# Queries' rests on GpSimd, the last tile's sums on VectorE, and first passes in front of the scores of their round

## The reference

```
h = ln(x, g1, be1);  x = attn(h, h, Wq1, Wk1, Wv1, Wo1, bo1) + x        # self attention, 1024 keys
h = ln(x, g2, be2);  x = attn(h, context, Wq2, Wk2, Wv2, Wo2, bo2) + x  # cross attention, 64 keys
h = ln(x, g3, be3);  a, gate = split(h @ Wp + bp)
x = a * gelu(gate) @ W2 + b2 + x

attn: 16 heads of 64; softmax(q k^T / 8) v, heads joined, @ Wo + bo
```

## Time and profile before

| | us |
|---|---|
| median of 3 runs | 1987.01 |
| profiled execution, own time | 1986.85 |
| its span, first to last instruction | 1985.1 |
| an ordinary chunk: score stage, products, slot | 9.27 + 7.09 + 3.14 |
| TensorE, VectorE, ScalarE, GpSimd busy | 1971.6, 1393.6, 1150.6, 1444.1 |

### The profile page before, as it was taken

The page is one execution under the profiler, slowest core; times in us unless marked ns, Lnnn a source line. Parts: engine busy times, 40 slices in busy tenths (PEclk is TensorE's granted clock), DMA queues, the critical chain, the costliest instruction groups (busy, mean ns, idle before and its releaser), DMA issues.

```text
span 1985.1 us, 32079 instructions
## 1 busy us (share of the span) xinstructions
PE 1971.6 (99%) x12056; PEld 1345.1 (68%) x12056; DVE 1393.6 (70%) x2382; ACT 1150.6 (58%) x2042; POOL 1444.1 (73%) x752
## 2 busy tenths in 40 slices
PE   9999999999999999999999999999999999999999
PEld 7555655667565556755655666565569999888888
DVE  6688687666768786587687666767867888744443
ACT  6665576565556665465666555656756766533332
POOL 3699899978979997899799798979896665200000
PEclk9999999999999999999999999999999999999999
DMA  7301000011000000020000001010030420000100
GB/s 256 138 38 64 17 22 22 12 33 54 22 12 12 33 12 33 1 75 11 11 12 22 33 12 54 22 33 1 22 106 22 150 65 1 1 22 33 33 11 32
DMA packets 40506, 77.63 MB, mean 39 GB/s; under 512 B 5920, under 2 KB 29600, under 8 KB 38304
## 3 DMA queue, kind: packets, MB, share of 16 engines
q1 hardware_dynamic: 40352, 75.59, 11.5%
HBM read 51.46 MB, written 24.12 MB: 38 GB/s over the span
## 4 chain that ended last, share of the span: by engine, by line
PE 92%; DVE 3%; POOL 3%; issue 1%; ACT 1%; POOLq 0%; DVEq 0%
PE score L577 21%; PE score L556 18%; PE score L703 9%; PE attn_project L512 8%; PE attn_project L688 5%; PE attn_project L717 5%; PE score L524 5%; PE score L658 4%; PE score L626 3%; PE attn_project L538 3%; PE first_score L538 3%; PE score L562 3%; POOL acc L1528 2%; PE first_score L672 1%; PE first_score L588 1%
## 5 line engine op out<-in xcount | busy, mean ns | idle before, releaser
L1528 POOL TENSOR_TENSOR acc<-acc,pT 128x1024 f32<-128x1024 f32 x384 | 916.7, 2387 | 54.4 <-POOL acc L1528 0.9
L1271 ACT ACTIVATE pT<-score 128x1024 f32<-128x1024 f32 x512 | 515.7, 1026 | 89.1 <-PE score L562 53.5
L556 PE MATMUL score<-qk 64*128 64x512 f32 x3072 | 467.5, 405 | 2.5 <-DVE hT L852 1.9
L577 PE MATMUL score<-pT,vT 128*64 128x512 f32 x1952 | 432.3, 595 | 0.0
L556 PEld LDWEIGHTS score<-qk 64*128 64x128 f32 x3072 | 267.2, 184 | 97.0 <-ACT pT L1271 20.9
L907 DVE TENSOR_REDUCE nmax<-first_score 128x2 f32<-128x1024 f32 x256 | 311.0, 1215 | 2.4 <-PE first_score L538 2.4
L907 DVE TENSOR_REDUCE nmax<-attn_project 128x2 f32<-128x1024 f32 x256 | 311.0, 1215 | 1.0 <-PE attn_project L538 0.9
L577 PEld LDWEIGHTS score<-pT,vT 128*64 128x64 f32 x1952 | 134.7, 137 | 259.5 <-issue 252.6
L1525 POOL TENSOR_TENSOR acc<-pT 128x1024 f32<-128x1024 f32 x64 | 153.4, 2396 | 68.6 <-ACT pT L1271 68.6
L512 PE MATMUL attn_project<-hT,wqk 128*128 128x512 f32 x738 | 186.3, 401 | 0.0
L703 PE MATMUL score<-hT,wp 128*128 128x512 f32 x768 | 183.7, 395 | 0.0
(11 more groups left out here) (201 smaller groups left out, 3007.2 us busy)
## 6 DMA issues: line engine op xcount, KB each, us to landing
wqk<-wqk_parts SPq DMA_DIRECT2D x24, 512.0 KB, 3.3
xres<-x_middle SPq DMA_DIRECT2D x10, 512.0 KB, 3.7
raw_v<-in_L_xattn_Wv SPq DMA_DIRECT2D x8, 512.0 KB, 4.9
keys_all<-keys SPq DMA_DIRECT2D x1, 4096.0 KB, 13.1
values_all<-values SPq DMA_DIRECT2D x1, 4096.0 KB, 13.2
wqk_parts<-wqk SPq DMA_DIRECT2D x8, 512.0 KB, 3.3
out_x<-xres SPq DMA_DIRECT2D x7, 512.0 KB, 3.0
xres<-in_x SPq DMA_DIRECT2D x3, 1024.0 KB, 5.7
```

Source lines behind the costliest of these rows:

```text
L556: last = e.matmul(bank, key_part(P, h, r, jt), queries1[P % 2][r, w, c * BANK:(c + 1) * BANK], start=(fresh and part == 0), stop=(not fres ...
L577: last = e.matmul(banks[bank][head * DH:(head + 1) * DH, :], vT[:, v_slot(D, jt), c0:c0 + DH], pT[:, jt, head, :], start=(jt == 0), stop=( ...
L1271: e.activation(pT[:, jt].rearrange("p h n -> p (h n)"), SC[R % 2][:, :], ACT.Exp).then_inc(s.exponential, 1)
L1528: e.tensor_tensor(total, total, pT[:, jt], ALU.add).then_inc(s.probs_added, 1)
```

## The change

- **First passes.** Each round issues its first pass of the next chunk in front of its scores, where it issued it behind them. The passes themselves, their banks and the number of row maxima stay.
- **Queries' rests.** But for the first three units, ScalarE copies the scaled projection of the queries in fp32 from PSUM to SBUF, into the place that their rest will take, and this copy alone frees bank PJ. One chunk later ScalarE rounds it from SBUF (round_queries, between the shift and write_oT), and GpSimd subtracts in place (split_queries, at the end of its chunk). VectorE no longer takes part. The whole keys are kept in the place of their rests too, where a tile of their own held them.
- **The last tile's sums.** GpSimd adds seven tiles with six additions. VectorE folds the eighth tile by itself (fold_last, behind the transposes of the maxima, in front of fold_sums). The product that sums over partitions takes both, 64 columns, and VectorE adds the two halves (totals) in front of the reciprocals.

```diff
         maxima = sb("maxima", [PART, 2, SQUARE])
-        keys_full = sb("keys_full", [PART, BANK // 2])
         QB = BANK // SQUARE
         quads = sb("quads", [PART, PART])
-        folded = sb("folded", [PART, 2 * QB])
+        folded = sb("folded", [PART, 3, 2 * QB])
+        totals = sb("totals", [PART, 2 * QB])
         rsum = sb("rsum", [PART, QB])
...
             ("wo1", [PAIRS, DIM], F32R))
+        _, qk1_whole, _, qk0_whole = overlay(
+            ("before_qk", [PRING * N + 3 * TILES * BANK + (2 * ARING + 1) * BANK], F32), ("qk1_whole", [4 * N + BANK], F32),
+            ("sums_between", [2 * BANK], F32), ("qk0_whole", [4 * N + BANK], F32))
         PAIR = BANK // 2
+        queries_whole = [tile[:, N:2 * N] for tile in (qk0_whole, qk1_whole)]
+        keys_whole = [tile[:, 2 * N:3 * N].rearrange("p (c n) -> p c n", c=CHUNKS) for tile in (qk0_whole, qk1_whole)]
         queries1 = [tile[:, 0:2 * N].rearrange("p (w n) -> p w n", w=2) for tile in (qk0, qk1)]
...
         keys_of = numbered((P, u) for P in range(B * PAIRS) for u in range(CHUNKS))
+        queries_of = numbered((P, u) for P in range(B * PAIRS) for u in range(2, 2 + CHUNKS))
+        FIRST_QUERIES = [(0, 2), (0, 3), (1, 2)]
+
+        def queries_rest(unit):
+
+            if unit in FIRST_QUERIES:
+                return s.first_queries_lo, queries_of[unit]
+            return s.queries_lo, queries_of[unit] - len(FIRST_QUERIES)
...
             return jobs + [("out1", *tile, through[i % len(through)]) for i, tile in enumerate(out1_tiles(C))]
+
+        def queries_unit(C):
+
+            P, c = divmod(C, CHUNKS)
+            return [(P + 1 + c, 3 - c)] if C >= 0 and P + 1 + c < B * PAIRS else []
...
                 last.then_inc(s.qk_projected, 1)
-                free[bank] = ((s.split_lo, qk_of[P, u]),)
+                free[bank] = ((s.split_lo, keys_of[P, u]) if u < 2 else queries_rest((P, u)) if (P, u) in FIRST_QUERIES
+                              else (s.queries_kept, queries_of[P, u] - len(FIRST_QUERIES)),)
...
                 bank = PASS_BANKS[head][half]
-                need.wait_ge(s.split_hi, qk_of[P, 2 + c])
+                need.wait_ge(s.queries_hi, queries_of[P, 2 + c])
                 need.wait_ge(s.keys_rounded, keys_of[P, half])
...
                 if part < len(TERMS):
-                    for u in (2 + c, jt // TPC):
-                        need.wait_ge(s.split_hi, qk_of[P, u])
-                        need.wait_ge(s.split_lo, qk_of[P, u])
+                    need.wait_ge(s.queries_hi, queries_of[P, 2 + c])
+                    need.wait_ge(*queries_rest((P, 2 + c)))
+                    need.wait_ge(s.split_hi, keys_of[P, jt // TPC])
+                    need.wait_ge(s.split_lo, keys_of[P, jt // TPC])
                     if part == 0:
...
                 need.wait_ge(s.acc_folded, C + 1)
+                need.wait_ge(s.last_folded, C + 1)
                 need.wait_ge(s.quads_made, 4)
                 bank_free(bank)
-                e.matmul(banks[bank][:, 0:2 * QB], quads[:, :], folded[:, :], start=True, stop=True
-                         ).then_inc(s.summed, 1)
-                free[bank] = ((s.sum_inverted, C + 1),)
+                both = folded[:, 0:2] if C % 2 == 0 else folded[:, 0:3:2]
+                e.matmul(banks[bank][:, 0:4 * QB], quads[:, :], both, start=True, stop=True).then_inc(s.summed, 1)
+                free[bank] = ((s.sum_totalled, C + 1),)
...
                         sum_quads(C - 1, "T0")
+                    if C + 1 < NC:
+                        for head in range(2):
+                            first_score(*next_part(C + 1, jt), head)
                     for part in range(len(TERMS) + (jt % TPC < 2)):
...
                             score(TILES * C + jt, part, head)
-                    if C + 1 < NC:
-                        for head in range(2):
-                            first_score(*next_part(C + 1, jt), head)
                 for jt in range(TILES):
...
+            def fold_last(C):
+
+                need.wait_ge(s.exponential, TILES * (C + 1))
+                need.wait_ge(s.summed, C - 1 if C > 1 else 0)
+                e.tensor_reduce(folded[:, 1 + C % 2], pT[:, TILES - 1].rearrange("p h (b n) -> p (h b) n", n=SQUARE), AX.X,
+                                ALU.add, apply_transpose=True).then_inc(s.last_folded, 1)
+
             def fold_sums(C):
-                need.wait_ge(s.probs_added, (TILES - 1) * (C + 1))
+                need.wait_ge(s.probs_added, ADDS * (C + 1))
                 need.wait_ge(s.summed, C)
-                e.tensor_reduce(folded[:, :], acc[:, C % ARING].rearrange("p h (b n) -> p (h b) n", n=SQUARE), AX.X, ALU.add,
+                e.tensor_reduce(folded[:, 0], acc[:, C % ARING].rearrange("p h (b n) -> p (h b) n", n=SQUARE), AX.X, ALU.add,
                                 apply_transpose=True).then_inc(s.acc_folded, 1)
...
                 need.wait_ge(s.summed, C + 1)
+                e.tensor_reduce(totals[:, :], banks[bank][:, 0:4 * QB].rearrange("p (w q) -> p q w", w=2), AX.X, ALU.add
+                                ).then_inc(s.sum_totalled, 1)
+                need.wait_ge(s.sum_totalled, C + 1)
                 for head in range(2):
                     r = slice(head * DH, (head + 1) * DH)
-                    last = e.reciprocal(rsum[r, :], banks[bank][r, head * QB:(head + 1) * QB])
+                    last = e.reciprocal(rsum[r, :], totals[r, head * QB:(head + 1) * QB])
                 last.then_inc(s.sum_inverted, 1)
...
                 for job in jobs:
-                    if job[0] == "qk":
-                        split_qk(*job[1:])
+                    if job[0] == "qk" and job[2] < 2:
+                        change_keys(*job[1:])
                     elif job[0] == "sum":
...
                     turn_max(C + 1)
+                if C + 1 < NC:
+                    fold_last(C)
                 if C == NC - 1:
...
                 if u >= 2:
-                    e.activation(queries1[P % 2][:, 0, (u - 2) * BANK:(u - 1) * BANK], banks[bank], ACT.Copy, scale=SCALE
-                                 ).then_inc(s.split_hi, 1)
+                    span = slice((u - 2) * BANK, (u - 1) * BANK)
+                    if (P, u) in FIRST_QUERIES:
+                        e.activation(queries1[P % 2][:, 0, span], banks[bank], ACT.Copy, scale=SCALE
+                                     ).then_inc(s.queries_hi, 1)
+                    else:
+                        e.activation(queries_whole[P % 2][:, span], banks[bank], ACT.Copy, scale=SCALE
+                                     ).then_inc(s.queries_kept, 1)
                     return
                 need.wait_ge(s.keys_changed, keys_of[P, u] - 1)
-                e.copy(keys_full[:, :], banks[bank][:, 0:PAIR]).then_inc(s.keys_copied, 1)
+                e.copy(keys_whole[P % 2][:, u, PAIR:], banks[bank][:, 0:PAIR]).then_inc(s.keys_copied, 1)
                 e.copy(keys_hi[P % 2][:, u, PAIR:], banks[bank]).then_inc(s.keys_rounded, 1)
...
                 e.copy(keys_hi[P % 2][:, u, 0:PAIR], banks[bank][:, PAIR:]).then_inc(s.split_hi, 1)
+
+            def round_queries(P, u):
+                span = slice((u - 2) * BANK, (u - 1) * BANK)
+                need.wait_ge(s.queries_kept, queries_of[P, u] - len(FIRST_QUERIES))
+                e.copy(queries1[P % 2][:, 0, span], queries_whole[P % 2][:, span]).then_inc(s.queries_hi, 1)
...
                     need.wait_ge(s.attended, R - TILES + 1)
-                    need.wait_ge(s.probs_added, (TILES - 1) * (R // TILES - 1) + max(jt, 1))
+                    need.wait_ge(s.probs_added, ADDS * (R // TILES - 1) + min(max(jt, 1), ADDS))
+                    if jt == TILES - 1:
+                        need.wait_ge(s.last_folded, R // TILES)
                 e.activation(pT[:, jt].rearrange("p h n -> p (h n)"), SC[R % 2][:, :], ACT.Exp
...
                     make_shift(C + 1)
+                for unit in queries_unit(C - 1):
+                    round_queries(*unit)
                 write_oT(C)
...
+            def split_queries(P, u):
+                span = slice((u - 2) * BANK, (u - 1) * BANK)
+                need.wait_ge(s.queries_hi, queries_of[P, u])
+                e.tensor_tensor(queries1[P % 2][:, 1, span], queries_whole[P % 2][:, span],
+                                queries1[P % 2][:, 0, span].bitcast(F32), ALU.subtract).then_inc(s.queries_lo, 1)
+
             def add_probs(R):
...
                 for jt in range(1, TILES):
-                    add_probs(TILES * C + jt)
+                    if jt <= ADDS:
+                        add_probs(TILES * C + jt)
...
                         scale_oT(C - 3 + jt // 2)
+                for unit in queries_unit(C - 1):
+                    split_queries(*unit)
             for i in range(NT + 3):
...
```

(33 more changed lines are left out.)

## The result

The changed kernel takes 1989.34 us (median of 20 runs, 1988.69 to 1990.76); the kernel before took 1986.69 beside it (20 runs, 1985.15 to 1988.60). The ratio is 1.0015, 95% interval 1.0008 to 1.0022: 0.15% slower by the medians, inside the 0.2% that the prediction counts as no change, though the interval lies above 1. I had said 2018 us, 1.6% slower, with 2001 as the lower end. The profiled execution has a span of 1987.0 against 1985.1, own time 1988.76.

What follows compares the result with a forecast made beforehand. VectorE's train of row maxima was taken to set the score stage. Terms 21.6 + 2.7 + 3.6 + 0.4 + 2.5 + 1.0 - 0.8 = 31.0 us on 1986.85 gave 2018 us, range 2001 to 2030.

Steps and rivals of the forecast that it cites:

- The second exponential is 0.43 late, and so is each behind it: Ordinary score stage, ScalarE's loop: claimed the delay carries through every later exponential to the products' bank, taken as 0.45 us.
- at each place in the stream the needed maximum is one later: Score stage, TensorE's order: between successive scores the first pass now waits for a maximum one later, +1.13 us.
- Train of maxima 0.69 earlier: Start of the score stage: without the queries' rest on VectorE, the row maxima start 0.69 us earlier.
- Ordinary stages 48 x 0.45 = 21.6: 48 ordinary score stages of the first attention: each 0.45 us longer from the new order, 21.6 us in all.
- After norm transposes 2.7: Six score stages after norm transposes: same chain behind the keys' last piece, 0.45 us each, 2.7 us in all.
- After output products 3.6: Six score stages after output products: 0.8 us later, of which 0.2 falls into slack; 0.6 each, 3.6 us.
- The sums' product, 2.5: Matrix product for the sums, 64 columns instead of 32: 0.04 us in each of 61, 2.5 us in all.
- The split of Wo1, 0.4: Chunks 1 to 4, where this split stands in front of VectorE's reduction: about 0.1 us each.
- The last two stages are TensorE's own work and the change leaves them alone: Products with the values and projections of each chunk: claimed unchanged at 7.09 and 3.14 us.
- Only F0's own place counts: Rival, score stages: only ScalarE's loop moves, 0.23 us in each of 62; total 2005 us, chance 0.13.
- no difference: Rival, whole kernel: the two halves cancel, total within 0.2%; chance 0.07.
- The faster rival: Rival, ordinary score stages: the earlier train of maxima takes stalls out, stage falls to 9.08 us; total 1978 us, chance 0.13.

## Why the prediction was wrong

**The step that failed** is how the delay reaches the end of the stage: "The second exponential is 0.43 late, and so is each behind it; the products' bank is the one that the seventh exponential frees." The first half holds. The second exponential starts 2.96 after the stage's start (887.92 - 884.96) against 2.42 before, the last 9.55 against 9.08. But the kernel before didn't end its stage on an exponential. Its last first pass F7 stood behind the last scores and was held by the sixth maximum; the products' weights followed it directly, 0.42 later, with the seventh exponential over at 890.50. The end of that stage in the timeline of the kernel before:

```profile
890.39 0.19 PEld L538 LDWEIGHTS attn_project<-qk 64*128 64x128 f32 x2 [0.27 <-DVE nmax L907]
890.40 0.49 PE L538 MATMUL attn_project<-qk 64*128 64x512 f32 x2
...
890.82 0.20 PEld L577 LDWEIGHTS score<-pT,vT 128*64 128x64 f32 x4 [0.24 <-issue]
```

In the new order F7 waits for the same maximum, and S7 stands behind it: from F7 to the products are 1.30 us (893.12 to 894.42). The step "at each place in the stream the needed maximum is one later" holds in front of S1 to S7 and not at the end of the stage, where the same maximum is the last one needed in both orders. So the end of the stage moves by 1.30 - 0.42 = 0.88, not by a maximum's 1.13. Less the earlier start of the train, 0.67, that leaves 0.21, where I had taken 0.45. Two kernels bear it out. With the start of the first maximum in, the stage of before is 1.91 + 6.87 + 0.06 + 0.42 = 9.26, and in the new order start + 6.87 + 0.06 + 1.30:

| kernel, stage | first maximum starts at | worked out | measured |
|---|---|---|---|
| order alone, chunk 37 | 1.94 | 10.17 | 10.17 |
| after, chunk 37 | 1.24 | 9.47 | 9.46 |
| after, chunk 35 (output products) | 1.13 | 9.36 | 9.34 |

(6.87: five maxima at 1.131 us and the sixth's 1.215.) I fitted the two tails, 0.42 and 1.30, to chunk 37 of before and of after; the other two rows are the test.

**Point by point.**
- Train of maxima 0.69 earlier: right (0.67). Second first pass held by the keys' change: right. Needed maximum one later for each round's scores: right; for the end of the stage not.
- Ordinary stages 48 x 0.45 = 21.6: measured 9.4, 0.20 each. After norm transposes 2.7: measured 0.32 and 0.20 in turn, 1.6. After output products 3.6: measured 6 x 0.26 = 1.6. There VectorE starts at 1.13, earlier still than the 1.2 to 1.3 I took. All three are the failed step.
- The last three stages, forecast 0: -0.42, -0.55 and +0.24, with 0.48 more in the slot of chunk 61, where F0 waits for ScalarE to copy the products out of the bank that it writes. They nearly cancel.
- The sums' product, 2.5: its group grew by 1.7 us of busy time, but ordinary slots are 3.11 against 3.14, so nothing of it shows. The totals (0.23 us each) and the second fold (ends at 860.36, products at 862.18) are covered, as forecast; the 1.0 for totals was not needed.
- The split of Wo1, 0.4: with the passes behind the scores it costs 3.4 us of span against the version that has it behind the fold (1.67 + 1.58 of it in the slots of chunks 1 and 2), and 5.8 with the sums' edit alone. In the changed kernel 0.8 of it is left, in the slot of chunk 3, where the split takes 2.58; in chunks 1 and 2 the splits fall so that they take 1.03 and 0.99, and the folds end before the products do. The forecast missed this price, and that the result hardly shows it is luck of timing.
- GpSimd idle for over 1 us a chunk: right, its wait in front of the first addition of a chunk grows from 68.6 to 155.1 us over the kernel.
- The tail, -0.8: right; the wait of the earlier trace rows falls from 1.08 to 0.20:

```profile
1482.92 1.09 PE L694 MATMUL first_score<-ident,probs 128*128 128x128 f32 x8 [0.20 <-POOL probs L1620]
```

- **Not in the sum at all**: where the tiles lie. It takes 8.3 us off the span of the kernel before: 3.9 behind the first attention, 6.2 in the slots and the start (1.5 of these by the shorter splits of Wo1), against 1.7 more in the score stages. The premise that failed here is "The last two stages are TensorE's own work and the change leaves them alone", and the sum has no term for the feed-forward part either. With all tiles in the new places, the rest of the change makes the kernel some 10 us slower (1976.7 to 1987.0), 0.5%: the sign I forecast, a third of the size.

| step | span | difference |
|---|---|---|
| kernel before | 1985.1 | |
| its tiles in the new places | 1976.7 | -8.3 |
| with the queries' rests and the sums | 1968.2 | -8.5 |
| with the new order: the kernel after | 1987.0 | +18.8 |

**The rivals.** "Only F0's own place counts" had the stage's price nearly right (0.23), for another reason: 0.22 is what F0 costs where ScalarE's loop is the bound, as the run with that pass alone in front shows, and not what happens in the changed kernel, whose passes wait for maxima. The faster rival described the parts other than the order: without it the stages fall to 9.09, as that rival said. That "no difference" came true is a coincidence: the two halves of the work leave +10 (+18.8 and -8.5), and only the -8 of the tiles' places, which no part of the prediction names, brings it to +1.9.

## What to carry to other kernels

Before carrying a delay through to the end of a stage, find the instruction that ends it now and what holds that one: where the same hold ends the stage in both orders, a reordering costs the work that stands behind it after, less the work behind it before, and not the period of the loop. When an engine is relieved, look for the next thing in its queue that was cheap by luck (here a split in front of a fold, 0.65 to 2.9 us long by where it falls against GpSimd's additions). A change that adds or drops a tile moves others, so run the kernel before once with its tiles in the new places ahead of crediting or blaming the edit.

## What the runs showed of the hardware that was not expected

- The pace of TensorE's 512-column matmuls on hT depends on where tiles lie in SBUF: 395 against 390 ns and 401 against 398 in the groups above, the granted clock 1.00 in both. Over the kernel it is 7 to 8 us, three times over (1986.6 to 1978.6, of which 1.5 is the splits', 1978.1 to 1971.2, 1975.5 to 1967.9). The cause inside the chip is not shown.
- VectorE's subtraction of two 128x512 tiles of SBUF (the split of Wo1) takes 0.65 to 2.9 us in these runs; where it begins during a GpSimd addition, it ends 0.55 us behind that addition's end in the two pairs shown.
- Behind an idling of 2.27 us in a score stage the mean granted clock of the products was 0.82, behind one of 1.62 it was 1.00 (queries' rests alone, chunks 5 and 7).
- A weight load for the products starts 0.08 us before the modelled end of the last matmul of the scores; a bank freed in time is worth 0.05 us a stage there, no more.
